# Where one projection and four statistics stand at the end of a fused FFN, attention, FFN kernel

## Chip, cores and metric

The kernel runs on one core of a Trainium2 chip. The metric is the device time of one execution in microseconds (us), the median of several runs. Engines by their short names: PE is TensorE, PEld its weight loads, DVE VectorE, ACT ScalarE, POOL GpSimd, SP SyncE, which issues most of the DMAs.

## What is computed

4096 tokens of width 128 pass through half an FFN, an attention over a memory of 4096 keys and values, and half an FFN again, each behind a layer norm:

```
x = x + 0.5 * ffn(layernorm(x))          # 8 experts, top 2, hidden 176, and a shared expert
x = x + attn(layernorm(x))
x = x + 0.5 * ffn(layernorm(x))

def attn(h):
    q = h @ Wq.T + bq
    probs = softmax(q @ keys.T / sqrt(128))     # 4096 keys
    return (probs @ values) @ Wo.T + bo
def layernorm(x):
    return (x - mean(x)) / sqrt(var(x) + 1e-5)
```

## The kernel before, in words

**Tiling.** The tokens are 32 tiles of 128, taken in 8 groups of 4 tiles. X stays in SBUF the whole time. The attention works in 16 **units**, u = 0 to 15 (LAST is 15): unit u is group u // 2 against one half of the keys (2048). One engine program is written by hand for each engine: all of them loop over the units and, in a unit, over 8 **halves** h = 0 to 7. H = 8u + h counts halves through the attention. Nothing but semaphores ties the engines together, and each engine works through its own list strictly in order, so an instruction that waits holds up all behind it on its engine.

**One half of a unit.** In half h PE makes the scores of tile h // 2 against 1024 keys (six products of 512 columns, L1501 to L1503) into one of three pairs of score banks (banks 0 to 5). DVE takes the maximum (L1218), ACT the exponentials (L847, for a tile kept for PE L856). Three of a unit's four tiles (two in units 0 and 15) are transposed without PE: DVE transposes 32x32 squares (E, L1213), and DMAs issued by SP and ACT move them into probsT (L387). The other tiles are transposed by PE (L1525).

**Rings.** 16 chunks of keys make 8 **rings** of a unit, two chunks each; ring r belongs to unit r // 8. From ring 6 on these steps belong to ring r, with the half in which each engine's program has them: PE transposes the own tiles into bank TB (H = r + 12, `transpose_pair`); ACT copies the moved part into p_hi (H = r + 10, `moved_high`, L822) and POOL takes p_lo, what the copy lost (same H, `moved_low`, L612); ACT does the same for PE's tiles (H = r + 11, `own_high`, L806) and DVE their p_lo (H = r + 13, `own_low`, L1206); PE multiplies by the values (H = r + 14, `values`, L1546 to L1548). There is one bank TB, so the transposes of ring r + 1 wait for `own_low(r)`. `moved_high(r)` waits for `values(r - 3)`, since p_hi has three slots. In the last unit the odd rings use another bank than TB. From H = 127 on PE puts a half's transposes ahead of its values, and there are no scores any more.

**A unit's end.** When all values of unit w are in, ACT copies them (`copy_oT`), PE multiplies by Wo (`project_out(w)`, L1556, at H = 8w + 23), into TB except for unit 14, ACT copies that to y (`copy_y`, L871), and POOL adds y, weighted, to X (`add_block`, L628 and L633). For unit 13 these stand at H = 127 on PE, at H = 125 in ACT's list, and in half 4 of the stretch after unit 15 on POOL (H = 132).

**Layer norms.** They have numbers n: 16 (SECOND_LN) is the second FFN's for group 0, 17 for group 1, and so on. DVE does `moments_of(n, g)`: `statistics` (four BN_STATS of X, L963) and `aggregate` (MEMSET and four BN_AGGR, L971 and L973). POOL does `inverse_deviation(n)` (neg_mean L514, var_eps L515, rstd L517) and `normalize` (xn, L524); for n = 18 DVE does the latter (`normalize_early`, L993). moments and neg_mean are single buffers, so the two engines hand them back and forth:

```python
# DVE, aggregate(n)
dve.wait_ge(stats_done, n + 1)
wait(dve, moments_read, 2 * n)          # POOL has read the moments of n - 1
dve.memset(settled[:, :], 0.0)
# POOL, inverse_deviation(n)
pool.wait_ge(moments_done, moments_before(n) + 1)
pool.tensor_tensor(neg_mean[:, :], moments[:, :, 0], minus_one[:, :], ALU.mult).then_inc(moments_read, 1)
pool.tensor_tensor(var_eps[:, :], moments[:, :, 1], eps[:, :], ALU.add).then_inc(moments_read, 1)
```

**Early parts of the second FFN.** PE transposes xn of norm 16 into TB at H = 125, of norm 17 into bank 1 at H = 130, of norm 18 into bank 0 at H = 133 (`transpose_x`, L1283, after `early_gate`, L1295). DVE routes group 0's tokens from H = 134 on, while the last rings run.

Of the kernel before, what the change touches and what calls it, by code (L numbers as in the profile page):

```python
# [15 lines left out]
GT = 4  # L16
# [19 lines left out]
UNITS = 2 * GROUPS  # L36
# [67 lines left out]
def macaron_kernel(nc: bass.Bass, x, wup, wdown, gate_w, expert_bias, shared_up, shared_down,  # L104
                   wq, bq, wo, bo, keys_values, out):
    with ExitStack() as ctx:
# [216 lines left out]

        def projection_bank(w):

            return result_banks[1] if w == LAST - 1 else TB

        def early_logits(i):

# [141 lines left out]
        def _(pool):  # L471
# [171 lines left out]
            for u in range(UNITS + 2):  # L643
                g = u // 2
                for h in range(HALVES):

                    ring = pair_at(u * HALVES + h + 4)
                    if ring is not None:
                        moved_low(ring)
                    if has_next_group(u, u % 4) and h == 0:  # L650
                        inverse_deviation(g + 1 + ATTENTION_LN)
                        normalize(g + 1 + ATTENTION_LN, g + 1)
                    if u < UNITS and u % 2 == 1 and h == 1:
                        add_bias(g)
                    if 2 <= u < LAST and h == ADD_HALF:
                        add_block(u - 2)
                    if u == LAST + 1 and h == 4:
                        add_block(LAST - 2)
                    if u == LAST - 1 and h == 1:
                        inverse_deviation(SECOND_LN)  # L660
                        normalize(SECOND_LN, 0)
                    if u == LAST - 1 and h == 5:
                        inverse_deviation(SECOND_LN + 1)
                    if u == LAST and h == 3:
                        normalize(SECOND_LN + 1, 1)
                    if u == LAST and h == 4:
                        inverse_deviation(SECOND_LN + 2)
                    if u == LAST + 1 and h == 4:
                        inverse_deviation(SECOND_LN + 3)
# [4 lines left out]
        def _(act):  # L674
# [192 lines left out]
            def copy_y(w):  # L867

                act.wait_ge(out_proj_done, w + 1)
                wait(act, block_added, w)  # L870
                act.activation(y[:, :, :].rearrange("p t d -> p (t d)"), projection_bank(w), ACT.Copy  # L871
                               ).then_inc(y_copied, 1)
# [10 lines left out]
            for u in range(UNITS + 2):  # L883
                g = u // 2
                prepares = u % 2 == 1 and u < LAST
                for h in range(HALVES):
# [55 lines left out]
                    if ring:  # L942
                        moved_high(ring)
                    w = projection_at(H + 2)
                    if w is not None:
                        copy_y(w)
                    if 2 <= u and u % 2 == 0 and h == 1:
                        shift_exponentials(g - 1)
            ffn(1)
# [3 lines left out]
        def _(dve):  # L953
# [22 lines left out]
            def moments_of(n, g):  # L976
                statistics(n, g)
                aggregate(n)
# [250 lines left out]
            for u in range(UNITS + 2):  # L1229
                g = u // 2  # L1230
                prepares = u % 2 == 1 and u < LAST
                for h in range(HALVES):
# [19 lines left out]
                        merge_shifts(g - 1)  # L1252
                    if 2 <= u and u % 2 == 0 and h == 5:
                        merge_shares(g - 1)
                    if u == LAST - 1 and h in (0, 4):
                        moments_of(SECOND_LN + h // 4, h // 4)
                    if u == LAST and h == 1:
                        moments_of(SECOND_LN + 2, 2)
                    if u == LAST + 1 and h == 1:
                        moments_of(SECOND_LN + 3, 3)  # L1260
                    if u == LAST + 1 and h in (3, 4):
                        normalize_early(SECOND_LN + 2, 2, 2 * (h - 3), h == 4)
# [16 lines left out]
        def _(pe):  # L1279
# [288 lines left out]
            for u in range(UNITS + 2):  # L1568
                g = u // 2
                prepares = u % 2 == 1 and u < LAST  # L1570
                for h in range(HALVES):
# [6 lines left out]
                    if w is not None:  # L1578
                        if w == LAST - 1:
                            pe.wait_ge(exp_done, 2 * GT * UNITS)  # L1580
                        else:
                            wait(pe, p_lo_done, filled)
                        project_out(w)
                    if prepares and h == Q_HALF:
                        wait(pe, p_lo_done, filled)
                        transpose_for_q(g + 1, TB)
# [14 lines left out]
                    if u == LAST + 1 and h == 5:  # L1601
                        early_gate(1)
                        pe.wait_ge(normalized, SECOND_LN + 3)
                        transpose_x(banks[:, 0, :])
                    if u == LAST + 2 and h == 0:
                        early_gate(2)
# [3 lines left out]
                    for step in (2, 0) if H >= UNITS * HALVES - 1 else (0, 2):  # L1610
                        ring = pair_at(H + step)
                        if ring is None:
                            continue
                        if step == 0:
                            values(ring)
                            continue
                        if w is not None and w < LAST - 1:
                            pe.wait_ge(y_copied, w + 1)
                        if ring == UP:
                            pe.wait_ge(y_copied, 1)  # L1620
                        if prepares and h == Q_HALF:
                            pe.wait_ge(xT_copied, g + 2 + ATTENTION_LN)
                        if prepares and h == Q_HALF + 1:
                            pe.wait_ge(q_ready, g + 2)
                        if u == LAST and h == Q_HALF:
                            pe.wait_ge(xT_copied, SECOND_LN + 1)
                        if u == LAST and h == Q_HALF + 1:
                            pe.wait_ge(expz_done, GROUPS + 1)
                        transpose_pair(ring)
            ffn(1)  # L1630


# [51 lines left out]
```

## Time and profile before

| | us |
|---|---|
| median of 3 runs | 636.55 (635.56 to 638.65) |
| the profiled execution | 636.61 |
| its span in the trace | 634.8 |
| busy in the span: PE | 599.1 (94%) |
| DVE | 528.3 (83%) |
| ACT | 454.0 (72%) |
| POOL | 415.5 (65%) |

The span is what the trace covers; 1.8 us of the profiled execution's time lie around it. Start times below are us from the span's start. A matmul's printed duration is longer than the distance to the next, since matmuls overlap. The granted clock of PE is 1.00 of its 2.4 GHz level in all parts shown.

### The profile page before, as it was taken

What the parts mean: (1) busy time and instruction counts of PE and PEld (TensorE: products, weight loads), DVE (VectorE), ACT (ScalarE), POOL (GpSimd) and SP (SyncE); (2) the same over time, 40 slices, a digit from 0 to 9 for tenths busy, and PEclk for the clock granted to TensorE, in tenths of its full rate; (3) what the DMA queues carried; (4) which work ended last, traced back from release to release, by engine and by line L of the source; (5) the groups of instructions that cost most, each with busy time, mean ns of one, the idle gap of its engine ahead of it and who ended that gap; (6) DMA issues with size and microseconds to landing.
All of it is one profiled execution on the core that took longest, in us unless ns stands there. A gap on an engine that the chain in (4) does not pass through costs nothing.

```text
span 634.8 us, 10665 instructions
## 1 busy us (share of the span) xinstructions
PE 599.1 (94%) x3508; PEld 443.4 (70%) x3508; DVE 528.3 (83%) x913; ACT 454.0 (72%) x756; POOL 415.5 (65%) x484
## 2 busy tenths in 40 slices
PE   7799989899899999999999999999999999899987
PEld 3466656567677777777877778777787767566655
DVE  5899886988977978978887897897888858899884
ACT  3577776576777867767777776776877786488886
POOL 4868980564476865966768687596678887536520
PEclk9999999999999999999999999999999999999999
DMA  8012120425447274473744727446374460000001
GB/s 310 13 34 68 35 68 1 128 65 124 117 99 172 56 170 106 95 162 75 161 99 103 169 60 170 106 94 158 76 162 89 115 133 1 1 2 35 36 18 50
DMA packets 36118, 59.28 MB, mean 93 GB/s; under 512 B 9312, under 2 KB 9952, under 8 KB 35936
## 3 DMA queue, kind: packets, MB, share of 16 engines
q1 hardware_dynamic: 31808, 52.82, 33.9%
q10 hardware_dynamic: 3744, 4.74, 3.0%
q0 software_dynamic: 512, 1.05, 0.6%
q8 instruction: 28, 0.46, 0.3%
q14 instruction: 26, 0.21, 0.1%
HBM read 8.25 MB, written 2.10 MB: 16 GB/s over the span
## 4 chain that ended last, share of the span: by engine, by line
PE 57%; DVE 16%; POOL 10%; issue 9%; SPq 3%; ACT 3%; ACTq 0%; DMA 0%; POOLq 0%; DVEq 0%
PE banks L1501 7%; PE banks L1502 7%; PE banks L1503 7%; PE banks L1546 7%; PE banks L1548 7%; PE banks L1547 7%; PE banks L1525 4%; DVE bank_max L1218 4%; SPq L387 3%; DVE E L1213 3%; POOL xn L524 3%; DVE probsT L1100 2%; PE banks L1556 2%; PE banks L1358 2%; PE banks L1343 1%
## 5 line engine op out<-in xcount | busy, mean ns | idle before, releaser
L612 POOL TENSOR_TENSOR p_lo<-probsT,p_hi 128x768 fp32r<-128x768 f32 (+1 forms) x128 | 226.7, 1776 | 119.6 <-ACT p_hi L822 119.1
L1218 DVE TENSOR_REDUCE bank_max<-banks 128x1 f32<-128x1024 f32 x128 | 155.9, 1219 | 30.5 <-PE banks L1503 29.7
L822 ACT ACTIVATE p_hi<-probsT 128x768 fp32r<-128x768 f32 (+1 forms) x128 | 104.4, 816 | 28.2 <-PE banks L1548 24.4
L1501 PE MATMUL banks<-kv_lo,q_parts 128*128 128x512 f32 x256 | 111.6, 436 | 4.1 <-ACT E L847 1.8
L1213 DVE STREAM_TRANSPOSE E<-E 128x1024 f32<-128x1024 f32 x92 | 113.5, 1234 | 0.4
L1100 DVE SCALAR_TENSOR_TENSOR probsT<-banks,E 128x1024 bf16<-128x1024 f32 x80 | 96.0, 1218 | 20.9 <-PE banks L1343 19.6
L847 ACT ACTIVATE E<-banks,neg_max 128x1024 f32<-128x1024 f32 x92 | 102.4, 1113 | 10.4 <-DVE neg_max L1224 8.0
L1546 PE MATMUL banks<-p_hi,kv_lo 128*128 128x512 f32 x256 | 107.6, 420 | 1.4 <-issue 1.1
L720 ACT ACTIVATE probsT<-probsT 128x1024 bf16<-128x1024 bf16 x96 | 92.1, 981 | 17.9 <-DVE probsT L1100 14.8
L1548 PE MATMUL banks<-p_hi,kv_hi 128*128 128x512 f32 x256 | 102.3, 400 | 0.0
L1547 PE MATMUL banks<-p_lo,kv_hi 128*128 128x512 f32 x256 | 102.2, 399 | 0.0
L1502 PE MATMUL banks<-kv_hi,q_parts 128*128 128x512 f32 x256 | 101.4, 396 | 0.0
L1503 PE MATMUL banks<-kv_hi,q_parts 128*128 128x512 f32 x256 | 101.0, 394 | 0.0
L806 ACT ACTIVATE p_hi<-banks 128x256 fp32r<-128x256 f32 (+1 forms) x128 | 52.3, 408 | 62.5 <-PE banks L1525 62.3
L1206 DVE TENSOR_TENSOR p_lo<-banks,p_hi 128x256 fp32r<-128x256 f32 (+1 forms) x128 | 56.1, 438 | 30.6 <-ACT p_hi L806 30.2
L1358 PEld LDWEIGHTS banks<-wdown_b,probsT 128*128 128x128 bf16 x704 | 42.8, 98 | 27.8 <-ACT probsT L720 17.2
L1358 PE MATMUL banks<-wdown_b,probsT 128*128 128x128 bf16 x704 | 52.7, 220 | 5.9 <-ACT probsT L720 5.6
L1546 PEld LDWEIGHTS banks<-p_hi,kv_lo 128*128 128x128 f32 x256 | 48.3, 189 | 14.0 <-issue 3.4
L1501 PEld LDWEIGHTS banks<-kv_lo,q_parts 128*128 128x128 f32 x256 | 48.3, 189 | 13.1 <-ACT E L847 3.6
L1548 PEld LDWEIGHTS banks<-p_hi,kv_hi 128*128 128x128 f32 x256 | 48.1, 188 | 12.3
L1547 PEld LDWEIGHTS banks<-p_lo,kv_hi 128*128 128x128 f32 x256 | 48.2, 188 | 11.8 <-issue 1.7
L1503 PEld LDWEIGHTS banks<-kv_hi,q_parts 128*128 128x128 f32 x256 | 48.1, 188 | 11.6
(133 smaller groups left out, 935.5 us busy)
## 6 DMA issues: line engine op xcount, KB each, us to landing
probsT<-E SPq DMA_DIRECT2D x208, 128.0 KB, 2.4
probsT<-E SPq DMA_DIRECT2D x232, 64.0 KB, 2.0
probsT<-E ACTq DMA_DIRECT2D x72, 64.0 KB, 2.1
E<-in_keys_values SPq DMA_DIRECT2D x8, 512.0 KB, 3.5
out<-X SPq DMA_DIRECT2D x8, 256.0 KB, 2.0
X<-in_x SPq DMA_DIRECT2D x1, 1280.0 KB, 9.0
probsT<-E POOLq DMA_DIRECT2D x16, 64.0 KB, 2.4
X<-in_x SPq DMA_DIRECT2D x3, 256.0 KB, 5.3
```

Source lines behind the costliest of these rows:

```text
L612: pool.tensor_tensor(moved_part(p_lo, ring), moved_pair(ring // UP, ring % UP), moved_part(p_hi, ring).bitcast(fp32), ALU.subtract).then_i ...
L822: act.activation(moved_part(p_hi, ring), moved_pair(ring // UP, ring % UP), ACT.Copy).then_inc(moved_hi_done, 1)
L1100: dve.scalar_tensor_tensor(hidden[:, k, :, :], up_banks[PAIR_BANK[k]], 0.0, spread.unsqueeze(1).to_broadcast([P, 2, N]), ALU.max, ALU.mult ...
L1213: dve.transpose(half, half).then_inc(squares_done, 1)
L1218: dve.tensor_reduce(bank_max[:, i % 2, h:h + 1], score_pair(u, i, h).rearrange("p b n -> p (b n)"), AX.X, ALU.max).then_inc(bank_max_done, 1)
L1358: last = pe.matmul(result_banks[G % 2][:, t * D:(t + 1) * D], hidden[:, k, c % 2, t * P:(t + 1) * P], wdown_b[:, c, :], start=(c == 0 and ...
L1501: pe.matmul(bank, qh, kl, start=True, stop=False)
L1502: pe.matmul(bank, ql, kh, start=False, stop=False)
L1503: pe.matmul(bank, qh, kh, start=False, stop=True).then_inc(scores_done, 1)
L1546: pe.matmul(OB, vl, hi, start=(c == 0), stop=False)
L1547: pe.matmul(OB, vh, lo, start=False, stop=False)
L1548: pe.matmul(OB, vh, hi, start=False, stop=(c == KC - 1)).then_inc(pv_done, 1)
```

## The change

Four edits, all near the end of the attention.

1. Unit 13's projection goes to bank 0, a score bank, and not to TB. In PE's list it moves behind the transposes of ring 115 and the values of ring 113 in the same half (H = 127). It waits for all exponentials but the last two, where it waited for `own_low(114)`; the transposes of ring 115 no longer wait for `copy_y(13)`.
2. `copy_y(13)` moves in ACT's list from H = 125 to H = 130, and `transpose_x` into bank 0 (H = 133) waits for it as well.
3. `moments_of(16)` and `moments_of(17)` move in DVE's list from halves 0 and 4 of unit 14 to halves 4 and 6. POOL's `inverse_deviation(16)` with `normalize(16)` moves from half 1 to half 5 of unit 14, and `inverse_deviation(17)` from half 5 to half 7.
4. `moments_of(19)` moves on DVE from H = 129 to H = 130, behind `own_low(117)`.

```diff
-            return result_banks[1] if w == LAST - 1 else TB
+            return result_banks[1] if w == LAST - 1 else banks[:, 0, :] if w == LAST - 2 else TB
...
-                    if u == LAST - 1 and h == 1:
+                    if u == LAST - 1 and h == 5:
                         inverse_deviation(SECOND_LN)
                         normalize(SECOND_LN, 0)
-                    if u == LAST - 1 and h == 5:
+                    if u == LAST - 1 and h == 7:
                         inverse_deviation(SECOND_LN + 1)
...
-                    if w is not None:
+                    if w is not None and w != LAST - 2:
                         copy_y(w)
+                    if u == LAST + 1 and h == 2:
+                        copy_y(LAST - 2)
...
-                    if u == LAST - 1 and h in (0, 4):
-                        moments_of(SECOND_LN + h // 4, h // 4)
+                    if u == LAST - 1 and h in (4, 6):
+                        moments_of(SECOND_LN + h // 2 - 2, h // 2 - 2)
...
-                    if u == LAST + 1 and h == 1:
+                    if u == LAST + 1 and h == 2:
                         moments_of(SECOND_LN + 3, 3)
...
-                        else:
+                        elif w < LAST - 2:
                             wait(pe, p_lo_done, filled)
-                        project_out(w)
+                        if w != LAST - 2:
+                            project_out(w)
...
                         pe.wait_ge(normalized, SECOND_LN + 3)
+                        pe.wait_ge(y_copied, LAST - 1)
                         transpose_x(banks[:, 0, :])
...
-                        if w is not None and w < LAST - 1:
+                        if w is not None and w < LAST - 2:
                             pe.wait_ge(y_copied, w + 1)
...
                         transpose_pair(ring)
+                    if w == LAST - 2:
+
+                        pe.wait_ge(exp_done, 2 * GT * UNITS - 2)
+                        project_out(w)
```

DVE in halves 6 and 7 of unit 14, before (the rows begin behind the shares of the merge; p_lo is `own_low`, of rings 105 and 106):

```order
L1206 TENSOR_TENSOR p_lo<-banks,p_hi 128x256 [waits p_hi_done]
L1218 TENSOR_REDUCE bank_max<-banks 128x1 [waits scores_done]
L1213 STREAM_TRANSPOSE E<-E 128x4x256 [waits exp_done]
L1206 TENSOR_TENSOR p_lo<-banks,p_hi 128x256 [waits p_hi_done]
L1218 TENSOR_REDUCE bank_max<-banks 128x1 [waits scores_done]
```

and in the changed kernel:

```order
L1208 TENSOR_TENSOR p_lo<-banks,p_hi 128x256 [waits p_hi_done]
L1220 TENSOR_REDUCE bank_max<-banks 128x1 [waits scores_done]
L1215 STREAM_TRANSPOSE E<-E 128x4x256 [waits exp_done]
L965 BN_STATS stats<-X 128x6 [waits block_added,moments_done]
L965 BN_STATS stats<-X 128x6 x3
L973 MEMSET settled 128x1 [waits moments_read,stats_done]
L975 BN_AGGR moments<-stats 128x2 x4
L1208 TENSOR_TENSOR p_lo<-banks,p_hi 128x256 [waits p_hi_done]
```

The statistics of norm 17 now stand between ring 105's and ring 106's p_lo, with their wait for moments_read.

POOL from unit 14's beginning to half 7, before (L612 is `moved_low`; the first x3 are rings 101 to 103):

```order
L612 TENSOR_TENSOR p_lo<-probsT,p_hi 128x768 [waits moved_hi_done] x3
L514 TENSOR_TENSOR neg_mean<-moments,minus_one 128x4 [waits normalized,moments_done]
L515 TENSOR_TENSOR var_eps<-moments,eps 128x4
L517 TENSOR_TENSOR rstd<-var_eps,minus_half 128x4 [waits moments_read]
L524 TENSOR_SCALAR xn<-X,neg_mean,rstd 128x128 [waits xT_done,rstd_done]
L524 TENSOR_SCALAR xn<-X,neg_mean,rstd 128x128 x3
L612 TENSOR_TENSOR p_lo<-probsT,p_hi 128x768 [waits moved_hi_done] x4
L514 TENSOR_TENSOR neg_mean<-moments,minus_one 128x4 [waits normalized,moments_done]
L515 TENSOR_TENSOR var_eps<-moments,eps 128x4
```

and in the changed kernel:

```order
L612 TENSOR_TENSOR p_lo<-probsT,p_hi 128x768 [waits moved_hi_done] x7
L514 TENSOR_TENSOR neg_mean<-moments,minus_one 128x4 [waits normalized,moments_done]
L515 TENSOR_TENSOR var_eps<-moments,eps 128x4
L517 TENSOR_TENSOR rstd<-var_eps,minus_half 128x4 [waits moments_read]
L524 TENSOR_SCALAR xn<-X,neg_mean,rstd 128x128 [waits xT_done,rstd_done]
L524 TENSOR_SCALAR xn<-X,neg_mean,rstd 128x128 x3
L612 TENSOR_TENSOR p_lo<-probsT,p_hi 128x768 [waits moved_hi_done]
L628 TENSOR_TENSOR attended<-attended,share 128x512 [waits merge_b,y_copied]
L633 TENSOR_TENSOR X<-X,attended 128x512 [waits block_added,bias_added,y_scaled]
L612 TENSOR_TENSOR p_lo<-probsT,p_hi 128x768 [waits moved_hi_done]
L514 TENSOR_TENSOR neg_mean<-moments,minus_one 128x4 [waits normalized,moments_done]
L515 TENSOR_TENSOR var_eps<-moments,eps 128x4
```

Norm 16's instructions stand where norm 17's stood, behind ring 107, and norm 17's now behind ring 109 and `add_block(12)`.

PE in half 127, behind the last scores, before:

```order
L1556 MATMUL banks<-wo_s,attended 128x128 [waits oT_copied,p_lo_done]
L1556 MATMUL banks<-wo_s,attended 128x128 x3
L1525 MATMUL banks<-ident,probs 128x128 [waits p_lo_done,y_copied]
L1525 MATMUL banks<-ident,probs 128x128
L1546 MATMUL banks<-p_hi,kv_lo 128x512 [waits moved_lo_done,p_lo_done]
```

and in the changed kernel:

```order
L1527 MATMUL banks<-ident,probs 128x128 [waits p_lo_done]
L1527 MATMUL banks<-ident,probs 128x128
L1548 MATMUL banks<-p_hi,kv_lo 128x512 [waits moved_lo_done,p_lo_done]
L1549 MATMUL banks<-p_lo,kv_hi 128x512
L1550 MATMUL banks<-p_hi,kv_hi 128x512
L1548 MATMUL banks<-p_hi,kv_lo 128x512
L1549 MATMUL banks<-p_lo,kv_hi 128x512
L1550 MATMUL banks<-p_hi,kv_hi 128x512
L1558 MATMUL banks<-wo_s,attended 128x128 [waits oT_copied,exp_done]
L1558 MATMUL banks<-wo_s,attended 128x128 x3
```

The transposes and six products with values go ahead of the projection, and nothing there waits for ACT's copy of y.

## Rows read from the trace of the kernel before

**Rows 1.** By stretch: length, busy (count) of PE, PEld, DVE, ACT, POOL; PE clock, DMA
```profile
488.00:514.40 26.40, 26.34 (x133) 20.67 (x133) 20.01 (x34) 18.80 (x34) 20.85 (x18) 1.00 0.52 120
514.40:549.80 35.40, 31.71 (x178) 23.90 (x177) 26.98 (x61) 20.72 (x41) 26.78 (x26) 1.00 0.20 45
```
**Rows 2.** Timeline, PE, end of unit 14: start, duration, engine, line, [idle before <-releaser]
```profile
487.77 1.16 PE L1556 MATMUL banks<-wo_s,attended 128*128 128x128 f32 x8 [0.76 <-DVE p_lo L1206]
```
**Rows 3.** Timeline, DVE, halves 4 to 7 of unit 14
```profile
479.88 0.83 DVE L963 BATCH_NORM_STATS2 stats<-X 128x6 f32<-128x128 f32 x4
...
481.05 0.39 DVE L1206 TENSOR_TENSOR p_lo<-banks,p_hi 128x256 fp32r<-128x256 f32 x1
...
486.17 1.23 DVE L1213 STREAM_TRANSPOSE E<-E 128x1024 f32<-128x1024 f32 x1
487.33 0.38 DVE L1206 TENSOR_TENSOR p_lo<-banks,p_hi 128x256 fp32r<-128x256 f32 x1
```
**Rows 4.** Timeline, POOL, halves 5 to 7 of unit 14
```profile
487.94 1.83 POOL L612 TENSOR_TENSOR p_lo<-probsT,p_hi 128x768 fp32r<-128x768 f32 x1 [1.29 <-ACT p_hi L822]
...
489.88 0.20 POOL L515 TENSOR_TENSOR var_eps<-moments,eps 128x4 f32<-128x4 f32 x1
...
497.76 1.83 POOL L612 TENSOR_TENSOR p_lo<-probsT,p_hi 128x768 fp32r<-128x768 f32 x1 [0.66 <-ACT p_hi L822]
```
**Rows 5.** Timeline, DVE, halves 1 to 5 of unit 15
```profile
496.36 0.87 DVE L963 BATCH_NORM_STATS2 stats<-X 128x6 f32<-128x128 f32 x4
...
497.98 0.42 DVE L1206 TENSOR_TENSOR p_lo<-banks,p_hi 128x256 fp32r<-128x256 f32 x1 [0.34 <-ACT p_hi L806]
498.32 1.21 DVE L1218 TENSOR_REDUCE bank_max<-banks 128x1 f32<-128x1024 f32 x1
```
**Rows 6.** Timeline, PE, halves 2, 3 and 5 of unit 15
```profile
499.26 0.38 PE L1525 MATMUL banks<-ident,probs 128*128 128x128 f32 x2
499.71 0.50 PE L1501 MATMUL banks<-kv_lo,q_parts 128*128 128x512 f32 x1
...
507.29 0.60 PE L1283 MATMUL banks<-ident,xn 128*128 128x128 f32 x4
```
**Rows 7.** Timeline, SP's DMA queue, moves of unit 14
```profile
483.99 19.47 SPq L387 DMA_DIRECT2D probsT<-E  x28
```
**Rows 8.** Timeline, PE, from H = 127 to the transposes of ring 120
```profile
514.39 1.05 PE L1556 MATMUL banks<-wo_s,attended 128*128 128x128 f32 x8
516.13 0.44 PE L1525 MATMUL banks<-ident,probs 128*128 128x128 f32 x2 [0.69 <-ACT attended L871]
...
522.58 0.44 PE L1525 MATMUL banks<-ident,probs 128*128 128x128 f32 x2 [0.62 <-DVE p_lo L1206]
...
526.29 0.30 PE L1525 MATMUL banks<-ident,E 128*128 128x128 f32 x1 [0.22 <-DVE p_lo L1206]
...
528.62 0.66 PE L1283 MATMUL banks<-ident,xn 128*128 128x128 f32 x4
```
**Rows 9.** Timeline, DVE, the same stretch; xn is one instruction, then both of a pair
```profile
515.85 0.15 DVE L1224 TENSOR_REDUCE neg_max<-bank_max 128x1 f32<-128x2 f32 x1
520.93 0.87 DVE L963 BATCH_NORM_STATS2 stats<-X 128x6 f32<-128x128 f32 x4
523.81 0.94 DVE L993 TENSOR_SCALAR xn<-X,neg_mean,rstd 128x128 f32<-128x128 f32 x1
526.06 2.48 DVE L993 TENSOR_SCALAR xn<-X,neg_mean,rstd 128x128 f32<-128x128 f32 x2
```
**Rows 10.** Timeline, POOL, the same stretch
```profile
522.84 1.82 POOL L612 TENSOR_TENSOR p_lo<-probsT,p_hi 128x768 fp32r<-128x768 f32 x1
525.40 3.06 POOL L612 TENSOR_TENSOR p_lo<-probsT,p_hi 128x768 fp32r<-128x768 f32 x2 [0.73 <-ACT p_hi L822]
```
**Rows 11.** Timeline, ACT, the same stretch
```profile
516.89 1.11 ACT L856 ACTIVATE probs<-banks,neg_max 128x1024 f32<-128x1024 f32 x1
521.56 0.84 ACT L822 ACTIVATE p_hi<-probsT 128x768 fp32r<-128x768 f32 x1 [0.31 <-PE banks L1548]
```

## The prediction

> **What bounds the kernel now.** I read the busy times by stretch first. In unit 15 PE works 26.34 of 26.40 us; from the last scores to the second FFN it works 31.71 of 35.40 [rows 1]. So ahead of 514.4 a delay of PE is paid in full and nothing can be won there but PE's own work; behind it there are holes to win, 3.7 us in all. Then the timelines, engine by engine. At the end of unit 14 PE has one hole, 0.76 us, in which `project_out(12)` waits for DVE's p_lo of ring 106 [rows 2]: there DVE is the late engine, and it runs without a gap from the statistics of norm 17 to that p_lo [rows 3]. After the last scores PE waits 0.69 for `copy_y(13)`, 0.62 for the p_lo of ring 117, which stands behind the statistics of norm 19, and 0.22 for the p_lo of ring 119 [rows 8, 9]. The changed lists are then laid over these rows by hand: each instruction starts when its engine is free and its semaphores are there.
>
> **Part 3 of the change, statistics of norms 16 and 17: two new waits.** Norm 16's statistics leave half 0, where PE had no hole, and take the place of norm 17's: that wins nothing. Norm 17's now follow the transpose of 486.17 and start at 487.33, where p_lo of ring 106 stood [rows 3]. They take 0.83, but `aggregate(17)` needs moments_read at 34, and the last count comes from POOL's var_eps of norm 16. That instruction now stands behind ring 107's p_lo, exactly where the trace has norm 17's: it ends at 489.88 + 0.20 = 490.08 [rows 4]. From the end of the statistics to the following p_lo it is 481.05 - 479.88 - 0.83 = 0.34 [rows 3]; so p_lo of ring 106 starts at 490.08 + 0.07 (a semaphore) + 0.30 = 490.45 and not at 487.33, **3.12 later**. `project_out(12)` is its first customer; PE loses 3.12. One thing softens it: POOL no longer computes norm 16 ahead of the merge of unit 14, DVE's small operations there wait less for POOL, and the chain up to ring 107 runs some 0.2 earlier. I take **+2.9** (bounds 2.7 and 3.2).
>
> The second wait: `aggregate(18)` on DVE (statistics at 496.36, [rows 5]) needs var_eps of norm 17, which now stands behind ring 109's p_lo on POOL. That one starts at 497.76 and ends at 499.59 [rows 4]; var_eps ends 0.32 behind it, as 490.08 does behind 487.94 + 1.83, at 499.91. With 0.07 + 0.30 as above, p_lo of ring 109 starts at 500.3 and not at 497.98. PE's transposes of ring 110 start 0.45 behind that, at 500.75, and not at 499.26 [rows 6]: 1.5 more. (All in times of before; the 2.9 is added to both sides, since ring 109's copy on ACT follows PE.) Behind these transposes PE had a hole of 499.71 - 499.26 - 0.14 = 0.31, a wait for the first exponential of unit 15, which itself waited for moved data. SP issues the 28 moves of that unit in one unbroken run from 483.99 to 503.46 [rows 7], and it starts at a transpose ahead of both waits: the data don't come later, and the hole closes: -0.3. Net **+1.2** (bounds 0 and 1.6).
>
> The third bite: DVE is now 2.3 + 2.9 late where PE is 4.1 late. From p_lo of ring 109 to that of ring 112 it has three p_lo, three maxima and three transposes, 0.42 + 1.21 + 1.23 each, every one starting 0.08 ahead of its predecessor's end, and a small one: about 8.05 [rows 3, 5]. That puts ring 112's p_lo at 511.3 and PE's `transpose_x` at 511.7, where its own delay would put it at 507.29 + 4.1 = 511.4 [rows 6]: **+0.3** (bounds 0 and 0.7). By half 126, where DVE idles over a microsecond, it has caught up. Sum of part 3: 2.9 + 1.2 + 0.3 = **+4.4**. ACT, POOL and DMA keep step with PE: ring 120's moves need 16 x 0.70 = 11.2 [rows 7] and still end over a microsecond before they are wanted.
>
> **Parts 1, 2 and 4, the tail** (times of before again). PE's transposes of ring 115 start at 514.39 and not 516.13 [rows 8]. The six products follow, then the projection from 516.0 to 516.9: it doesn't shrink, it only no longer keeps the ring chain waiting. ACT is rid of a copy of 0.6, and starts tile 3's exponentials once its neg_max is there, at 515.85 + 0.15, so at 516.05 for 516.89 [rows 9, 11]: 0.84 won, with the second one at 518.2. Ring 117's p_lo on DVE no longer waits for the statistics, and ring 118's transposes go at 520.9 for 522.58 [rows 8]: **1.7 won**. Now the statistics (0.87 and 0.34, as before) stand ahead of ring 118's p_lo: 522.4, ring 119's transposes 522.5.
>
> Here it is given back. DVE's next two instructions are norm 18's xn. The rows show what such an instruction does beside POOL's p_lo: the first took 0.94 and ended 0.09 behind POOL's instruction that ended at 524.66; a later pair took 2.48, while POOL ran two without a gap, and ended 0.08 behind the second [rows 9, 10]. In my schedule the pair starts at 522.35, inside POOL's p_lo of ring 118 (522.04 to 523.85); ACT's copy for ring 119 (0.84 long, [rows 11]) is done 0.3 earlier than that, so POOL goes on without a gap to 525.67. DVE's pair ends at 525.75, ring 119's p_lo at 526.1, and the transposes of ring 120 start at 526.15 for 526.29 [rows 8]. Won so far: 0.14; `transpose_x` into bank 0 follows at 528.5 for 528.62. `copy_y(13)`, now in ACT's list before ring 120's copy, is covered: DVE is at xn until about 527.3. From there everything keeps the order of before and comes 0.1 earlier. Tail: **-0.1** (bounds -1.6, if nothing is given back, and +0.5).
>
> Sum: +4.4 - 0.1 = **+4.3**. The profiled execution took 636.61, 0.06 above the median: 640.9. What a measurement of this kernel can tell from no change is about 0.5%, 3.2 us; so above 639.7 is slower.
>
> **A rule on the shared port.** The rows say that POOL's second instruction went ahead of a waiting DVE instruction. The Trainium skill, page "SBUF — State Buffer", section "Who interferes with whom", says that the engine that issues first gets the shared pair for its whole instruction and the other blocks fully. That an xn lasts until POOL's p_lo ends agrees with it (2.48 for two). Taken literally, DVE's second xn is issued before POOL's next p_lo and would go between them; that is rival A, and by it the sum would be about +3.
>
> **Rivals.**
>
> A. *The tail keeps its gain*: the second xn slips between POOL's instructions, ring 119's p_lo ends at 524.5, ring 120's transposes go 1.7 earlier, of which 1.4 are left where xn of the second pair is awaited. Total 4.4 - 1.4 = +3.0: 639.6. For it: the schedule hangs on 0.3 us. Against: the pair of 2.48. 0.13.
>
> B. *Only the first wait bites*: POOL gets to norm 17 sooner or DVE's lateness is absorbed in unit 15. +2.9 - 0.1 = +2.8: 639.4. Against: PE has no slack there [rows 1]. 0.10.
>
> C. *POOL is early enough, only the work of the statistics is added* ahead of ring 106's p_lo: 481.05 - 479.88 = +1.17 [rows 3], less the tail's 0.1: 637.7. It would need var_eps of norm 16 before 488.2, two microseconds earlier than [rows 4] have that place. 0.07.
>
> D. *Faster*: var_eps is there before 488.2 as in C, and DVE catches up within unit 14, since it was relieved of 1.17 in half 0, and the tail keeps its gain as in A: -1.5, 635.1. It decides at the same point, 488.2 against 490.08; and DVE's gapless run starts behind half 0. 0.04.
>
> E. *The tail is worse*: another DVE instruction falls behind a POOL one and the routing of group 0, which follows on DVE, slips by one p_lo, some 1.2: 642.1. 0.08.
>
> **The numbers.** My forecast has 0.58 and spans 639.9 to 641.9 by its bounds. The range 638.5 to 642.0 holds it, A and B, and leaves out C, D and half of E. Slower by over 0.5%: nearly all of the forecast (0.56), E (0.08), a little of A and B (0.04): 0.68. Faster: D without its edge, 0.03. The rest, 0.29, is within 0.5%.
>
> **What would show it.** In the changed profile: PE's hole before `project_out(12)` grows from 0.76 to about 3.7 and is put down to DVE's p_lo or its aggregate; DVE has a hole of about 1.9 between the BN_STATS and the BN_AGGR of norm 17, released by POOL's var_eps, and one of about 2.7 at norm 18; a new PE hole of about 1.5 before ring 110's transposes; the 0.69 after the last scores is gone; from the last scores to the second FFN's first product it takes about as long as before. I am wrong if DVE shows no wait for moments_read in unit 14, or if the time comes out under 638.

## The result, and the profile after

| | us |
|---|---|
| before, median of 6 runs | 637.23 (635.56 to 638.8) |
| changed kernel, median of 6 runs | 643.1 (641.95 to 644.34) |
| ratio, with its 95% interval | 1.0097 (1.0075 to 1.0119) |
| the changed kernel's profiled execution | 642.88, its span 641.0 |

The change makes the kernel 0.97% slower, 5.9 us, where 4.3 were forecast. The sign and the place are right; the time lies 1.1 us above the range.

Busy times by stretch in the changed kernel (length, then PE, PEld, DVE, ACT, POOL, the granted clock of PE, DMA share). The first two answer to [rows 1], the others cut the same time where it matters:

```profile
488.00:514.40 26.40, 21.96 (x98) 17.46 (x99) 17.42 (x39) 13.63 (x26) 18.98 (x19) 0.94 0.46 105
514.40:556.00 41.60, 37.65 (x212) 28.60 (x212) 30.83 (x67) 26.08 (x50) 31.89 (x31) 1.00 0.23 51
...
487.00:491.40 4.40, 0.51 (x3) 0.07 (x1) 2.37 (x12) 1.36 (x3) 3.28 (x5) 1.00 0.92 205
491.40:495.40 4.00, 3.98 (x14) 3.52 (x15) 2.41 (x3) 0.60 (x1) 1.99 (x5) 0.57 0.93 204
495.40:505.60 10.20, 9.29 (x43) 7.14 (x41) 4.93 (x16) 6.64 (x12) 7.02 (x7) 1.00 0.52 123
```

Between 488 and 514.4 PE worked 26.34 us before; now 21.96, and part of that at a clock of 0.57. The timeline of PE, by start and duration, with the idle time in brackets, answers to [rows 2, 6, 8]:

```profile
487.12 0.39 PE L1505 MATMUL banks<-kv_hi,q_parts 128*128 128x512 f32 x1
491.43 2.06 PE L1558 MATMUL banks<-wo_s,attended 128*128 128x128 f32 x8 [3.92 <-DVE p_lo L1208]
493.14 0.77 PE L1548 MATMUL banks<-p_hi,kv_lo 128*128 128x512 f32 x1
493.71 0.63 PE L1549 MATMUL banks<-p_lo,kv_hi 128*128 128x512 f32 x1
494.14 0.63 PE L1550 MATMUL banks<-p_hi,kv_hi 128*128 128x512 f32 x1
494.57 0.55 PE L1548 MATMUL banks<-p_hi,kv_lo 128*128 128x512 f32 x1
494.95 0.40 PE L1549 MATMUL banks<-p_lo,kv_hi 128*128 128x512 f32 x1
...
505.67 0.44 PE L1527 MATMUL banks<-ident,probs 128*128 128x128 f32 x2 [0.97 <-DVE p_lo L1208]
...
522.42 1.05 PE L1558 MATMUL banks<-wo_s,attended 128*128 128x128 f32 x8
523.31 0.38 PE L1527 MATMUL banks<-ident,probs 128*128 128x128 f32 x2
...
532.52 0.30 PE L1527 MATMUL banks<-ident,E 128*128 128x128 f32 x1 [1.77 <-DVE p_lo L1208]
...
534.85 0.66 PE L1285 MATMUL banks<-ident,xn 128*128 128x128 f32 x4
```

The hole ahead of `project_out(12)` is 3.92 and not 0.76. The eight instructions of the projection take 2.06 where they took 1.16, and the four products behind them start 0.43 to 0.57 apart; at full clock it is 0.24 (in the same execution, 494.95 to 495.19 for the last row and the product after it). A second hole of 0.97 stands ahead of ring 110's transposes. After the last scores the projection of unit 13 no longer holds anything, but ring 120's transposes wait 1.77.

DVE shows both waits, and POOL what ended them (timelines; answers to [rows 3, 4, 5]):

```profile
487.82 0.83 DVE L965 BATCH_NORM_STATS2 stats<-X 128x6 f32<-128x128 f32 x4
490.68 0.18 DVE L975 BATCH_NORM_AGGREGATE moments<-stats 128x2 f32<-128x6 f32 x1 [2.03 <-POOL var_eps L515]
...
490.98 0.39 DVE L1208 TENSOR_TENSOR p_lo<-banks,p_hi 128x256 fp32r<-128x256 f32 x1
...
501.60 0.87 DVE L965 BATCH_NORM_STATS2 stats<-X 128x6 f32<-128x128 f32 x4
504.92 0.06 DVE L973 MEMSET settled<- 128x1 f32 x1 [2.45 <-POOL var_eps L515]
...
528.62 3.42 DVE L995 TENSOR_SCALAR xn<-X,neg_mean,rstd 128x128 f32<-128x128 f32 x2
```

```profile
488.44 1.80 POOL L612 TENSOR_TENSOR p_lo<-probsT,p_hi 128x768 fp32r<-128x768 f32 x1 [1.04 <-ACT p_hi L822]
...
490.35 0.20 POOL L515 TENSOR_TENSOR var_eps<-moments,eps 128x4 f32<-128x4 f32 x1
...
502.63 1.84 POOL L612 TENSOR_TENSOR p_lo<-probsT,p_hi 128x768 fp32r<-128x768 f32 x1 [0.29 <-ACT p_hi L822]
...
504.60 0.19 POOL L515 TENSOR_TENSOR var_eps<-moments,eps 128x4 f32<-128x4 f32 x1
```

**An account by landmarks.** Distances within one execution are steadier here than the whole time. The program is the same up to unit 14, and still `project_out(11)` starts anywhere from 461.3 to 464.3 in the profiled executions of this study, by chance. A part of that may be the clock of the first 30 us (0.95 was granted in the changed kernel's execution, 1.00 before), but not all: at 1.00 there it is 461.3 (before) and 462.7 (e4_filled). So each kernel below is read between landmarks of PE: P11 and P12 are the starts of `project_out(11)` and `(12)`, S the end of the last scores, T the start of ring 120's transposes, X that of `transpose_x` into bank 0.

| kernel | P11 to P12 | P12 to S | S to T | T to X |
|---|---|---|---|---|
| before | 26.49 | 26.62 | 11.90 | 2.33 |
| changed | 29.37 | 29.35 | 11.74 | 2.33 |
| difference | +2.88 | +2.73 | -0.16 | 0 |

From X to the end it is 106.2 in both. The 0.8 that are left of the spans' 6.2 lie ahead of P11, where nothing was changed.

The landmarks have a spread of their own. `e1_tail_only`, `e6_xn_together` and `e7_projection_alone`, described below, have the program of before ahead of H = 125, and yet P11 to P12 is 26.43, 26.73 and 26.44 in them (before 26.49), and P12 to S 26.31, 26.28 and 26.31 (before 26.62; the 0.3 arises at H = 122). So a difference of 0.3 in one of these two columns can be chance, and the second column's +2.73 is rather 2.7 to 3.0.

### The profile page after: what moved, and what is told of

It is laid out like the page before. It is cut to its first block, busy times and chain, and to the rows that moved or that the text cites. A ratio compares the mean times of both kernels' runs of the same rounds, so it can differ in the third digit from the quotient of the medians.

```text
span 641.0 us, 10641 instructions
## 1 busy us (share of the span) xinstructions
PE 598.8 (93%) x3484; PEld 445.8 (70%) x3508; DVE 529.3 (83%) x913; ACT 454.0 (71%) x756; POOL 416.3 (65%) x484
## 3 DMA queue, kind: packets, MB, share of 16 engines
q0 software_dynamic: 512, 1.05, 0.6%
## 4 chain that ended last, share of the span: by engine, by line
PE 56%; DVE 16%; POOL 12%; issue 10%; ACT 3%; SPq 1%; DMA 1%; ACTq 0%; POOLq 0%; DVEq 0%
PE banks L1503 7%; PE banks L1504 7%; PE banks L1505 7%; PE banks L1548 7%; PE banks L1550 7%; PE banks L1549 7%; PE banks L1527 4%; DVE bank_max L1220 4%; POOL xn L524 3%; DVE E L1215 3%; DVE probsT L1102 2%; PE banks L1360 2%; PE banks L1558 2%; POOL kv_lo L603 1%; PE banks L1345 1%
## 5 line engine op out<-in xcount | busy, mean ns | idle before, releaser
L612 POOL TENSOR_TENSOR p_lo<-probsT,p_hi 128x768 fp32r<-128x768 f32 (+1 forms) x128 | 227.0, 1778 | 124.1 <-ACT p_hi L822 123.4
```

The lines of the kernel that those rows point to most:

```text
L612: pool.tensor_tensor(moved_part(p_lo, ring), moved_pair(ring // UP, ring % UP), moved_part(p_hi, ring).bitcast(fp32), ALU.subtract).then_i ...
```

## The experiments

All times are in us, medians; the kernel before, run beside them on the same chip, stood at 636.96 (first four), 637.19 (next four) and 636.99 (last two). Two theories stood: **the wait and the clock** (both waits as forecast, and a third term, PE's clock after a hole of 3.9 us), against **the place** (the moved instructions or the projection's new bank cost as such).

### Each part alone

`e1_tail_only` is the changed kernel with this undone:

```diff
-                    if u == LAST - 1 and h in (4, 6):
-                        moments_of(SECOND_LN + h // 2 - 2, h // 2 - 2)
+                    if u == LAST - 1 and h in (0, 4):
+                        moments_of(SECOND_LN + h // 4, h // 4)
...
-                    if u == LAST - 1 and h == 5:
+                    if u == LAST - 1 and h == 1:
                         inverse_deviation(SECOND_LN)
                         normalize(SECOND_LN, 0)
-                    if u == LAST - 1 and h == 7:
+                    if u == LAST - 1 and h == 5:
                         inverse_deviation(SECOND_LN + 1)
```

> The changed kernel with the statistics of norms 16 and 17, and POOL's share of them, put back where they were: only the projection, its copy and the statistics of norm 19 stay moved. Main theory: the whole loss is in what was put back, so this is within 0.3 us of the kernel before (637.1, minus 0.1). PE's waits for DVE's p_lo ahead of project_out(12) are 0.76 as before, the granted clock is 1.00 there, and DVE's first pair of xn in the tail takes over 3 us. Rival 1 (the projection in a score bank costs something too): 1 us or more above the kernel before. Rival 2 (the tail keeps its gain once PE isn't late): 1.4 us below the kernel before.

Measured: 636.58, ratio 1.0003 (0.9985 to 1.0022). The hole ahead of P12 is 0.76 again, P11 to P12 is 26.43, and S to T is 11.74 as in the changed kernel.

`e2_stats_only` is the kernel before with that part alone, so the same diff the other way round.

> The kernel before with only the statistics of norms 16 and 17 and POOL's share of them moved. Main theory: 5.5 to 6.0 us above the kernel before, as much as the whole change, with PE's hole of 3.9 us ahead of project_out(12), the granted clock at half for some 3.3 us behind it, and a second hole of 1.0 ahead of ring 110's transposes. Rival 1 (part of the loss comes from the projection's move): 4.5 us or less.

Measured: 642.56, ratio 1.0092 (1.0072 to 1.0112), and the hole of 3.92:

```profile
491.11 1.16 PE L1556 MATMUL banks<-wo_s,attended 128*128 128x128 f32 x8 [3.92 <-DVE p_lo L1206]
...
493.08 0.63 PE L1546 MATMUL banks<-p_hi,kv_lo 128*128 128x512 f32 x1
```

Here the clock fell a microsecond later, behind the projection and not with it (1.00 from 491 to 492, 0.73 in the next microsecond, then 0.50), and the slow products are other ones; P12 to S is 29.25, as in the changed kernel. The whole loss sits in the statistics; the projection's move costs nothing.

### Taking the wait away, and leaving the order

`e3_two_buffers`:

```diff
-        moments = sb("moments", [P, GT, 2], fp32)
+        moments = sb("moments", [P, 2, GT, 2], fp32)
...
-                wait(dve, moments_read, 2 * n)
+                wait(dve, moments_read, 2 * (n - 1))
...
-                    last = dve.bn_aggr(moments[:, t, :], stats[:, n % 2, t, :])
+                    last = dve.bn_aggr(moments[:, n % 2, t, :], stats[:, n % 2, t, :])
```

and POOL reads `moments[:, n % 2, :, ...]`.

> The changed kernel with two buffers for the moments, so that the aggregate of norm n waits for POOL's reads of norm n - 2 and no longer of norm n - 1. The order of all instructions is the changed one. Main theory (the loss is the wait of moments_read and what the clock does after it): only the statistics' own 1.2 us ahead of ring 106's p_lo are left, PE's hole there is 1.7 to 2.0 and not 3.9, none ahead of ring 110's transposes; 1.0 us above the kernel before (0.7 to 1.3) if the clock stays at 1.00, and up to 2.7 above it if a hole of 1.8 already brings the clock down. Rival (the place of the statistics or of POOL's instructions costs as such): 4 us or more above the kernel before.

Measured: 638.48, ratio 1.0021 (1.0005 to 1.0038). PE:

```profile
489.35 1.16 PE L1558 MATMUL banks<-wo_s,attended 128*128 128x128 f32 x8 [1.92 <-DVE p_lo L1208]
```

P11 to P12 is 27.39, 0.9 above before, and P12 to S is 26.34: no second hole, no slow products. Of 5.9 us, 1.5 are left by the medians (0.3 to 2.4 by the interval), 0.5 from P11 to X by the landmarks. That fits the statistics' own time ahead of ring 106's p_lo, 1.17 of DVE. The order of the instructions is the changed one, so their place as such costs no more than this; the rest is the wait and what follows it.

### The clock by itself

`e4_filled` and `e10_half_filled` keep DVE's wait (2.07 and 2.04 us in them) and change only what PE does meanwhile:

```diff
                     bank = score_pair(u, i, h)[:, k, :]
+                    if u == LAST - 1 and i == GT - 1 and h == 1 and k == 1:
+                        for _ in range(13):
+                            pe.matmul(bank, qh, kl, start=True, stop=True)
```

(6 in `e10_half_filled`).

> The changed kernel with 13 more products of 512 columns (0.24 us each, 3.1 us) in front of the last scores of unit 14, into the bank that these scores then fill: PE works through most of the hole ahead of project_out(12), and DVE's wait is as long as ever. Main theory (the third term of the loss is the granted clock after the hole): the clock stays at 1.00 there, project_out(12) takes 1.05 to 1.2 and not 2.06, and the time is 1.6 us below the changed kernel's (1.2 to 1.8), so 641.5. Rival (the slow products after the hole come from something else, such as the weight loads or data): no change, or 3 us more if the added products lie on the path.

> e4_filled with 6 added products and not 13: a hole of some 2.5 us is left ahead of project_out(12), between the 1.9 of e3_two_buffers, at which the clock stayed at 1.00, and the 3.9 of the changed kernel, behind which it was at half for 3 us. If the clock term depends on the hole's length, the clock may fall or not here; whichever it does, project_out(12) to the last scores takes 27.5 us (clock kept, as in e4_filled) or 29.3 (lost, as in the changed kernel), and nothing between by more than 0.5 us. Rival (the term isn't the clock but has a share in each microsecond of hole): some 28.4.

Measured: 641.3, ratio 1.0067 (1.0046 to 1.0089), and 642.66, ratio 1.009 (1.0068 to 1.0113).

| kernel | hole ahead of P12 | clock behind it | P12 to S |
|---|---|---|---|
| before | 0.76 | 1.00 | 26.62 |
| e4_filled | 0.93 | 1.00 | 27.52 |
| e3_two_buffers | 1.92 | 1.00 | 26.34 |
| e10_half_filled | 2.51 | 0.50 to 0.77 in four us | 29.34 |
| changed | 3.92 | 0.50 to 0.73 in four us | 29.35 |

PE in `e4_filled`, then in `e10_half_filled`:

```profile
492.60 1.16 PE L1561 MATMUL banks<-wo_s,attended 128*128 128x128 f32 x8 [0.93 <-DVE p_lo L1208]
...
505.02 0.44 PE L1530 MATMUL banks<-ident,probs 128*128 128x128 f32 x2 [0.76 <-DVE p_lo L1208]
```

```profile
491.42 1.54 PE L1561 MATMUL banks<-wo_s,attended 128*128 128x128 f32 x8 [2.51 <-DVE p_lo L1208]
492.61 0.77 PE L1551 MATMUL banks<-p_hi,kv_lo 128*128 128x512 f32 x1
```

The clock is the last number but two of a stretch's row; the first row is of `e4_filled`, the second of `e10_half_filled`:

```profile
493.00:494.00 1.00, 1.00 (x9) 0.95 (x9) 0.97 (x3) 0.21 (x1) 1.00 (x3) 1.00 0.97 209
493.00:494.00 1.00, 1.00 (x3) 0.75 (x3) 0.84 (x1) 0.59 (x1) 0.49 (x2) 0.50 0.91 207
```

Filling most of the hole with useless products takes 1.8 us off between P12 and S (0.2 of it because the second hole is 0.76 and not 0.97) and 1.8 off the time (643.1 to 641.3; the intervals of the two ratios overlap, so this rests on the traces above all). Filling a third of it takes nothing.

From P11 to X the gain of `e4_filled` is only 1.3, since P11 to P12 is 29.91 there, 0.5 above the changed kernel (`e10_half_filled`: 29.42). That half microsecond arises ahead of the added products, where the two programs are the same. In this execution one small operation of DVE, which takes 0.17 in the changed kernel, started 0.03 behind POOL's p_lo (471.94 to 473.78) and lasted until that was done:

```profile
471.97 1.83 DVE L1188 TENSOR_TENSOR shift<-lowest_neg,neg_max 128x8 f32<-128x8 f32 x1
```

The same happened in the profiled executions of e6 (1.86) and e8 (1.84), and it is the likely reason for e6's 26.73. The term isn't a share of each idle microsecond: the clock keeps its upper level or drops to its lower one, 2.4 or 1.2 GHz, and it costs what it lacks: in the changed kernel 4.0 us at a mean of 0.57 (491.4 to 495.4), so 0.43 x 4.0 = 1.7. The distances of the products say 1.6: the fifth product behind the projection starts 3.52 behind P12, where it was 1.94 before (487.77 to 489.71). The Trainium skill, page "TensorE: Matmul & The Clock Gate", section "HAM oscillation — how this bites in real kernels", describes just that: a wait throttles PE, and the next stretch of work starts at the low clock, at a cost of half the throttled time. The traces agree in the cost, and in the start for the changed kernel (0.52 in the first microsecond behind P12); in e2 that stretch began with a microsecond at 1.00.

### The second wait alone

`e5_second_wait` is the kernel before with one edit:

```diff
-                    if u == LAST - 1 and h == 5:
+                    if u == LAST - 1 and h == 7:
                         inverse_deviation(SECOND_LN + 1)
```

> The kernel before with one edit: POOL's inverse_deviation(17) stands in half 7 of unit 14 and not in half 5. That leaves the first wait out and keeps the second (aggregate(18) on DVE waits for var_eps of norm 17). Main theory: no hole but the old 0.76 ahead of project_out(12), a DVE wait of about 2.5 us between the BN_STATS and the aggregate of norm 18, a PE hole of 0.9 to 1.2 ahead of ring 110's transposes, the clock stays at 1.00, and the time is 1.2 us above the kernel before (1.0 to 1.5). Rival (the second wait bites only because the first made DVE late): no hole, no change.

Measured: 640.2, ratio 1.0035 (1.0016 to 1.0054); the medians differ by 3.0 us, the ratio says 2.2 (1.0 to 3.4). P11 to P12 is 26.46, P12 to S 28.60, clock 1.00. PE, then DVE:

```profile
504.13 0.44 PE L1525 MATMUL banks<-ident,probs 128*128 128x128 f32 x2 [1.80 <-DVE p_lo L1206]
```

```profile
503.39 0.06 DVE L971 MEMSET settled<- 128x1 f32 x1 [3.26 <-POOL var_eps L515]
```

The wait is real on its own, and larger than expected: 2.0 to 2.3 us (28.60 against 26.62 before, or 26.31 in e1) for 1.2. Its length hangs on ring 109's copy on ACT, which stands behind four DMA issues:

```profile
496.57 0.52 ACTq L387 DMA_DIRECT2D probsT<-E  x1
...
497.12 1.47 ACTq L387 DMA_DIRECT2D probsT<-E  x1
498.63 1.52 ACTq L387 DMA_DIRECT2D probsT<-E  x2
```

The four took 3.58 in all (496.57 to 500.15), 3.09 before (493.69 to 496.78) and 2.72 in the changed kernel (498.94 to 501.66), and the copy behind them follows the end of the last one each time. So 0.5 of the surprise lies here, and the changed kernel's smaller hole goes with the shortest issues; what is left isn't explained. SP issues its moves in the same microseconds; that the two queues hold each other up would fit, but wasn't tried.

### The tail

`e6_xn_together` is `e1_tail_only` with both pairs of norm 18's xn at H = 132:

```diff
-                    if u == LAST + 1 and h in (3, 4):
-                        normalize_early(SECOND_LN + 2, 2, 2 * (h - 3), h == 4)
+                    if u == LAST + 1 and h == 4:
+                        normalize_early(SECOND_LN + 2, 2, 0, False)
+                        normalize_early(SECOND_LN + 2, 2, 2, True)
```

> e1_tail_only with one more edit: both pairs of norm 18's xn stand on DVE behind ring 119's p_lo (H = 132), where the first pair stood ahead of it (H = 131). Main theory (the tail's gain is given back because that pair waits for POOL's p_lo, 3.4 us for two): ring 119's p_lo and ring 120's transposes come 1.6 us earlier after the last scores than in e1, all four xn end about 0.4 us later than in e1, PE's transpose_x into bank 0 is held by them and comes 0.9 us earlier, and the time is 0.9 us below e1 (0.6 to 1.2). Rival (something else on PE or ACT holds the tail): the xn move and the time is e1's within 0.3.

`e7_projection_alone` is `e1_tail_only` with norm 19's statistics back at H = 129.

> The kernel before with only the projection of unit 13 and its copy moved; all statistics as before, those of norm 19 at H = 129. Main theory: ring 117's p_lo again stands behind the statistics, so ring 118's transposes come some 0.8 us later than in e1, but the first xn pair is held by POOL until the same moment, and ring 120's transposes come at the same time as in e1 within 0.2 us. Time as e1 and as the kernel before, within 0.5 us. Rival (the statistics of norm 19 are what pays): 0.7 us or more above e1.

| kernel | S to T | T to X | S to X | time | ratio |
|---|---|---|---|---|---|
| before | 11.90 | 2.33 | 14.23 | | |
| e1_tail_only | 11.74 | 2.33 | 14.07 | 636.58 | 1.0003 (0.9985 to 1.0022) |
| e6_xn_together | 10.19 | 2.89 | 13.08 | 637.28 | 0.9999 (0.9984 to 1.0014) |
| e7_projection_alone | 11.00 | 2.34 | 13.34 | 636.94 | 0.9991 (0.9976 to 1.0007) |

The tail's differences are below what the times can tell; the landmarks decide. e6 shows the mechanism: with the xn out of the way ring 120's transposes come 1.55 earlier, and of that 0.99 are left at X, where PE now waits for the xn themselves. So the gain of the projection's move was indeed given back to the pair of xn behind POOL's p_lo. PE in e6, at X:

```profile
529.20 0.66 PE L1286 MATMUL banks<-ident,xn 128*128 128x128 f32 x4 [0.49 <-DVE xn L995]
```

e7 missed: I expected T where e1 has it, and it came 0.74 earlier. DVE in e7, then in e1:

```profile
523.85 0.39 DVE L1208 TENSOR_TENSOR p_lo<-banks,p_hi 128x256 fp32r<-128x256 f32 x1
525.19 0.42 DVE L1208 TENSOR_TENSOR p_lo<-banks,p_hi 128x256 fp32r<-128x256 f32 x1 [0.95 <-ACT p_hi L806]
525.53 1.21 DVE L995 TENSOR_SCALAR xn<-X,neg_mean,rstd 128x128 f32<-128x128 f32 x2
```

```profile
521.31 0.86 DVE L965 BATCH_NORM_STATS2 stats<-X 128x6 f32<-128x128 f32 x4
...
522.81 3.42 DVE L995 TENSOR_SCALAR xn<-X,neg_mean,rstd 128x128 f32<-128x128 f32 x2
```

POOL in e7:

```profile
527.12 3.08 POOL L612 TENSOR_TENSOR p_lo<-probsT,p_hi 128x768 fp32r<-128x768 f32 x2 [0.71 <-ACT p_hi L822]
```

In e7 the pair starts late in a p_lo of POOL that ends at 526.40, POOL then has a pause of 0.71, and the pair waits once and not twice: 1.21. So the fourth edit, norm 19's statistics one half later, turns a gain of 0.9 (14.23 to 13.34) into one of 0.16. This rests on a single profiled execution of e7; S to X is steady, though, 14.06 to 14.08 in all five kernels that have e1's tail.

### A version ahead of both

`e8_both_wins` adds to e6 the two buffers of e3 and moves norm 17's statistics to half 0 of unit 15 (norm 16's stay in half 0 of unit 14, as before; `inverse_deviation(17)` stands in half 7):

```diff
+                    if u == LAST - 1 and h == 0:
+                        moments_of(SECOND_LN, 0)
+                    if u == LAST and h == 0:
+                        moments_of(SECOND_LN + 1, 1)
```

> e6_xn_together with two buffers for the moments, and the statistics of norm 17 moved on to half 0 of unit 15, where DVE idles (POOL's part in half 7 of unit 14). Main theory: the old hole of 0.76 ahead of project_out(12) closes too, nothing new opens, and the time is 0.9 + 0.7 = 1.6 us below the kernel before (1.0 to 2.0), 7 us below the changed one. Rival (DVE is the bound in unit 14 whatever stands there): no gain over e6.

Measured: 636.14, 1.05 us below the kernel before where 1.6 was expected, ratio 0.9988 (0.9975 to 1.0001), not clear of no change. The tail's gain is there, but the hole ahead of P12 didn't close: it is still 0.75, although 1.2 us of work had left DVE there. A row of DVE and one of POOL say why:

```profile
484.66 1.10 DVE L1194 TENSOR_TENSOR part<-sums,shift_exp 128x8 f32<-128x8 f32 x1
482.09 3.65 POOL L612 TENSOR_TENSOR p_lo<-probsT,p_hi 128x768 fp32r<-128x768 f32 x2
```

An operation of 8 columns takes 1.10 and ends with a p_lo of POOL (485.74), which norm 16 on POOL had made late. `e9_pool_later` is e8 with one more edit:

```diff
-                    if u == LAST - 1 and h == 1:
+                    if u == LAST - 1 and h == 5:
                         inverse_deviation(SECOND_LN)
                         normalize(SECOND_LN, 0)
```

> e8_both_wins with POOL's inverse_deviation(16) and normalize(16) in half 5 of unit 14 instead of half 1. In e8 the merge's first small operation on DVE (part, L1194) took 1.10 us, since POOL was at the p_lo that norm 16 had made late; that ate what the statistics' leaving had won, and the 0.75 hole stayed. Theory: with POOL's norm 16 behind ring 107 that operation takes 0.15, ring 106's p_lo comes 1 us earlier, the hole ahead of project_out(12) closes, and from project_out(11) to project_out(12) it is 25.8 to 25.9 us where it was 26.5 (and 26.6 in e8). Time 0.7 below e8, 1.8 below the kernel before (1.2 to 2.2). Rival (the hole is the time that PE's scores and ACT's copies need, not DVE's): e8's 26.6 and its time.

Measured: 635.08, ratio 0.9974 (0.9956 to 0.9992). PE and DVE:

```profile
487.47 1.16 PE L1561 MATMUL banks<-wo_s,attended 128*128 128x128 f32 x8 [0.31 <-DVE p_lo L1208]
```

```profile
483.61 0.28 DVE L1194 TENSOR_TENSOR part<-sums,shift_exp 128x8 f32<-128x8 f32 x1
```

P11 to P12 is 25.66, 0.8 below before and 1.0 below e8 (at most 0.15 of that is the chance wait of 1.84 in e8's execution), and S to X 13.09, 1.1 below before. That is the only kernel of the study that is faster than the one before clear of noise: 1.9 us, and 8.0 faster than the changed one. POOL's share in half 5 is part of the change under study; it pays once the buffer that couples the two engines is doubled.

## Why the prediction was right and wrong

| step | forecast | measured |
|---|---|---|
| first wait (P11 to P12) | +2.9 | +2.88 |
| second wait, with its third bite | +1.5 | about +1.0 |
| PE's clock behind the first hole | not in the sum | +1.6 to +1.7 |
| tail (S to X) | -0.1 | -0.16 |
| sum | +4.3 | +5.45 by landmarks, +5.9 by the medians |

**The first wait** came as worked out from [rows 3, 4]: DVE's 2.03 for var_eps of norm 16 (1.9 forecast), PE's hole 3.92 (3.7). e3 shows that it is the semaphore on the moments.

**The second wait** is there too (2.45 on DVE, 2.7 forecast; PE's hole 0.97 where 1.5 stood). Its net is P12 to S, +2.73, less the clock's 1.7 (1.3 if e1's P12 to S stands for before). So this term was forecast 0.2 to 0.5 too high. Its parts can be followed in the starts of PE, changed against before: 1.1 is lost ahead of ring 110's transposes, 0.3 is won back at the scores behind them, as forecast, and `transpose_x` of norm 17 loses 0.2, the third bite (0.3 forecast). The forecast's rival B, in which the second wait is absorbed, is ruled out by e5, and by e4, where the clock stays up and P12 to S is still 0.9 above before. Its size isn't a constant: alone it is 2.0 to 2.3.

**The term that failed is one that the sum lacks.** The working takes the loss of PE as the length of its hole: "PE loses 3.12", and nothing behind it. Behind the hole PE ran over 3 us at half its clock, which cost another 1.6 to 1.7 us and which e4 and e10 set apart. The views that I had gave the granted clock in [rows 1], 1.00 throughout, and I read that as a constant and not as what a busy PE had been granted; no step asked what a hole of 3.7 us, five times as long as the longest of its kind in [rows 2], would do to it. With the term the forecast is 4.3 + 1.7 = 6.0, so 642.6. That this is so near the 643.1 measured is luck in part: the landmarks sum to 5.45, and what the second wait was forecast too high stands in for time that lies ahead of P11.

**The tail** went as worked out, xn pair included (3.42 for two; 522.35 to 525.75, so 3.40, forecast), and e6 shows the give-back. Rival A, in which DVE's second xn slips between POOL's instructions, is ruled out in this order. The rule of the Trainium skill's page "SBUF — State Buffer", section "Who interferes with whom", that the loser blocks for a whole instruction, agrees with these rows, and so does its rule that the first to issue goes first: in the changed kernel POOL's next p_lo starts at 530.13 and DVE's second xn at 530.19. What was wrong is the prediction's reading, on which rival A rests, that the second xn would be issued before POOL's next p_lo. What I didn't see is that the fourth edit is harmful in itself: e7.

Rivals C and D needed var_eps by 488.2; it came at 490.55 (a start ahead of P11 that is 0.8 late included). Rival E gave nearly the measured time (642.1) by the wrong mechanism: no further instruction fell behind POOL's.

## What to carry to other kernels

Ask of every step moved later which buffer it hands over and who must have emptied it: here 1.2 us of statistics cost 5.9 (1.7 of it the clock), since a single buffer of 8 numbers in a partition ties the list of DVE to that of POOL, and the counterpart had been moved behind a 1.8 us instruction. Price a new hole of PE at its length, and ask what the clock does behind it if the trace has no hole as long: here 1.92 us cost nothing more, 2.51 us another 1.6 to 1.8. Compare executions by distances between landmarks when the edit is worth less than the spread of the start, and undo the edits one by one: here the first two were worth 0.9 us in the trace, the fourth took 0.7 of it back, and the third cost 5.6 (e2).

## What the runs showed of the hardware

- A hole of 1.92 us left PE's clock alone (e3, 1.00), behind holes of 2.51 (e10) and 3.92 (changed kernel, e2) it fell to half, 0.50, and cost some 1.7 us. In e2 it fell a microsecond later than in the changed kernel, behind the same hole, at the same cost.
- The start of the same program varies: `project_out(11)`, ahead of which all kernels are alike, starts at 461.3 to 464.3, and the clock granted in the first 30 us ranges from 0.94 to 1.00.
- A DVE operation of 8 columns that started beside POOL's p_lo took up to 1.86 us (e6; 1.10 in e8), and the same ones 0.12 to 0.36 in other executions; the statistics (BN_STATS) take 0.83 to 0.88 in all of these traces, beside POOL's p_lo too.
- The same four DMA issues of ACT took 2.72 (changed kernel), 3.09 (before) or 3.58 us (e5). From before to e5 the copy behind them and POOL's p_lo, on which DVE's wait hangs, came later by as much: 9.06 to 9.56 and 9.99 to 10.49 behind P12.
